# Turning rows by DMA instead of on TensorE in the block loop of a pre-norm state-space and mixture-of-experts kernel

## The reference

```python
# x: (2, 4096, 512)
def ssm(x):                                       # x is the layer-normalised input
    s = sigmoid(silu(x @ s_w1.T + s_b1) @ s_w2.T + s_b2)
    u = (x @ B_w.T + B_b) * s                     # 128 states
    h[t] = h[t-1] @ A.T + u[t]                    # scan over 4096 steps
    y = h @ C_w.T + C_b + x @ D_w.T + D_b
    return y * sigmoid(x @ g_w.T + g_b)

def moe(x):                                       # x is the layer-normalised x1
    chosen = argmax(x @ gate_w.T)                 # 8 experts
    return x + x @ expert_w[chosen].T

x1 = x + ssm(layernorm(x))
out = x1 + moe(layernorm(x1))
```

## Time and profile before

| | us |
|---|---|
| median of 3 runs | 1006.66 (1006.65 to 1008.63) |
| the profiled execution | 1007.09 |
| its span in the profile | 1005.3 |
| PE busy | 966.4 (96%) |
| DVE, ACT, POOL busy | 674.9, 408.1, 402.1 |

### The profile page before, as it was taken

The page is one execution under the profiler, slowest core; times in us unless marked ns, Lnnn a source line. Parts: engine busy times, 40 slices in busy tenths (PEclk is TensorE's granted clock), DMA queues, the critical chain, the costliest instruction groups (busy, mean ns, idle before and its releaser), DMA issues. The chain is left out here.

```text
span 1005.3 us, 16387 instructions
## 1 busy us (share of the span) xinstructions
PE 966.4 (96%) x5009; PEld 792.6 (79%) x5010; DVE 674.9 (67%) x1655; ACT 408.1 (41%) x704; POOL 402.1 (40%) x522
## 2 busy tenths in 40 slices
PE   7999999999999999999999999999857999999995
PEld 6788888888888888888888888888646888888884
DVE  6677777777777777777777687776985444444442
ACT  5333333333333333333333332332546666666662
POOL 1041616345261634626163362615273333333332
PEclk9999999999999999999999999999979999999998
DMA  9051022121302212130221203112265555555441
GB/s 322 12 178 43 22 105 79 48 86 42 126 32 95 83 44 88 40 126 33 95 84 43 97 31 126 41 44 85 84 220 178 159 160 166 168 159 161 138 149 55
DMA packets 47324, 101.70 MB, mean 101 GB/s; under 512 B 5781, under 2 KB 6549, under 8 KB 47264
## 3 DMA queue, kind: packets, MB, share of 16 engines
q1 hardware_dynamic: 33680, 61.93, 19.1%
q0 software_dynamic: 10800, 33.70, 8.7%
q10 hardware_dynamic: 2784, 5.31, 1.6%
HBM read 64.85 MB, written 37.90 MB: 102 GB/s over the span
## 5 line engine op out<-in xcount | busy, mean ns | idle before, releaser
L412 POOL TENSOR_TENSOR y_biased<-y_biased,gate 128x512 f32<-128x512 f32 x60 | 91.3, 1521 | 144.4 <-DVE y_biased L764 144.4
L481 POOL DMA_INDIRECT out<-gate,ids x71 | 69.9, 984 | 153.9 <-DVE gate L1029 115.2
L1355 PE MATMUL y<-expert_hi,x1T_hi 128*128 x284 | 119.3, 420 | 3.9 <-DVE x1T_lo L1023 3.9
L1029 DVE TENSOR_TENSOR gate<-y,x_rows 128x512 f32<-128x512 f32 x71 | 49.1, 691 | 108.2 <-PE y L1355 108.2
L1355 PE MATMUL y<-expert_hi,x1T_lo 128*128 x284 | 112.7, 397 | 0.0
L1355 PE MATMUL y<-expert_lo,x1T_hi 128*128 x284 | 112.3, 395 | 0.0
L1065 PE MATMUL gates<-GwT_hi,xT_hi 128*128 128x512 f32 x256 | 104.8, 409 | 0.0
L1065 PE MATMUL y<-DwT_hi,xT_hi 128*128 128x512 f32 x256 | 101.9, 398 | 0.5 <-DVE gateT L696 0.5
L1066 PE MATMUL gates<-GwT_lo,xT_hi 128*128 128x512 f32 x256 | 100.8, 394 | 0.0
L1067 PE MATMUL gates<-GwT_hi,xT_lo 128*128 128x512 f32 x256 | 100.3, 392 | 0.0
L1067 PE MATMUL y<-DwT_hi,xT_lo 128*128 128x512 f32 x256 | 100.3, 392 | 0.0
(11 more groups left out here) (246 smaller groups left out, 2372.8 us busy)
## 6 DMA issues: line engine op xcount, KB each, us to landing
x_rows<-routed_rows SPq DMA_DIRECT2D x71, 258.0 KB, 2.6
x_in<-L_attn_x SPq DMA_DIRECT2D x32, 512.0 KB, 4.4
x_rows<-L_attn_x SPq DMA_DIRECT2D x32, 512.0 KB, 4.4
raw_weights<-L_ffn_expert_w ACTq DMA_DIRECT2D x5, 1024.0 KB, 7.3
raw_weights<-L_ffn_expert_w SPq DMA_DIRECT2D x3, 1024.0 KB, 8.9
routed_rows<-padrow SPq DMA_DIRECT2D x9, 258.0 KB
out<-gate,ids POOLq DMA_INDIRECT x71, 2.8
raw_weights<-L_attn_D_w SPq DMA_DIRECT2D x1, 1024.0 KB, 8.1
```

The costliest lines, as they stand in the source:

```text
L412: nc.gpsimd.tensor_tensor(yb[:, i, :], yb[:, i, :], gate[:, i, :], ALU.mult).then_inc(S_["gated"], 1)
L481: nc.gpsimd.indirect_dma_start(out=out_rows, out_offset=bass.IndirectOffsetOnAxis(ap=ids[m][:, 0:1], axis=0), in_=res[m], in_offset=None, ...
L1029: nc.vector.tensor_tensor(res[m], Y[m % 2][:], rows[m][:, 0:D], ALU.add).then_inc(S_["slot_result"], 1)
L1355: ins = nc.tensor.matmul(Y[m % 2][:], x2T[a][:, k, m % 2 * P:(m % 2 + 1) * P], flat[w][:, bass.ds(first + k * D, D)], start=(k == 0 and a ...
```

## The change

In the block loop, from block 1 on, neither x_norm nor x1 is turned on TensorE. Instead each tile of 128x512 fp32 values is split into two planes of 16-bit halves (`halves`, 128x1024, two buffers), an SP DMA transposes it (`flipped`, two buffers), ACT joins the planes again to fp32 (`joined`, two buffers), and the high part is taken from that on ACT, the low part on POOL. The split is on ACT for x and on DVE for x1. The x_norm buffer goes: the normalised rows are written over x_in. One sequence number runs through all transposes: in block b the four tiles of x1 of block b-1, then the four of x of block b+1. So the tiles 0 to 2 of xT are written in the block before, each as soon as the gates products have read it; tile 3 follows at the next block's start, its low part on DVE. Block 0's own rows and the x1 of block 15 are turned on TensorE as before. The state products now open a block.

```diff
             xin, xn = sb("x_in", [P, NT, D]), sb("x_norm", [P, NT, D])   # before
+            xin = sb("x_in", [P, NT, D])
+            halves = [sb(f"halves{q}", [P, 2 * D], u16) for q in range(2)]
+            flipped = [sb(f"flipped{q}", [P, 2 * KD, P], u16) for q in range(2)]
+            joined = [sb(f"joined{q}", [P, KD, P]) for q in range(2)]
+        def planes(tile):
+            return tile.bitcast(u16).rearrange("p (d h) -> p h d", h=2)
+        def turn_x1(b, i):
+            return 2 * NT * b + NT + i
+        def turn_x(b, i):
+            return 2 * NT * (b - 1) + i
# SP
+            def load_x(b, n):
+                if b == 1:
+                    sp.wait_ge(S_["xT_psum"], NT)
+                elif b > 1:
+                    sp.wait_ge(S_["x_halves"], NT * (b - 2) + 2 * (n + 1))
+                sp.dma_start(xin[:, 2 * n:2 * n + 2, :], x_t[n][b]).then_inc(S_["xin_loaded"], 16)
+            def flip(n, made, count):
+                sp.wait_ge(made, count)
+                wait(sp, S_["joined"], n - 1)
+                sp.dma_start_transpose(flipped[n % 2][:], halves[n % 2][:]).then_inc(turned[n % 2], 16)
-            for b in range(3, NBLK):
-                load_x(b)
-                load_residual(b - 1, (b - 1) % 2, (b - 1) // 2)
-            load_residual(LASTB, 1, LASTB // 2)
+            for b in range(NBLK):
+                if b > 0:
+                    for i in range(NT):
+                        flip_x1(b - 1, i)
+                for n in range(NB):
+                    if b < LASTB:
+                        flip_x(b + 1, 2 * n)
+                        flip_x(b + 1, 2 * n + 1)
+                    if b + 2 < NBLK:
+                        load_x(b + 2, n)
+                    if n == 0 and b > 1:
+                        load_residual(b, b % 2, b // 2)
# POOL
+            def low_x1(b, i):
+                pool.wait_ge(S_["x2T_hi"], NT * b + i + 1)
+                hi, lo = [h[:, :, i % 2 * P:(i % 2 + 1) * P] for h in turned_rows(b, i)]
+                nc.gpsimd.tensor_tensor(lo, joined[turn_x1(b, i) % 2][:], hi.bitcast(f32), ALU.subtract
+                                        ).then_inc(S_["x2T_lo_pool"], 1)
+            # low_x(b, i): the same for xT
                 if b < LASTB:
                     rstd1(b + 1)
+                if b > 0:
+                    low_x1(b - 1, 0)
+                    low_x1(b - 1, 1)
+                    low_x1(b - 1, 2)
                 if b >= 2:
                     scatter(b - 2, q)
+                if b > 0:
+                    low_x1(b - 1, 3)
+                if b < LASTB:
+                    low_x(b + 1, 0)
                 if b > 0:
                     rstd2(b - 1, 1 - q)
+                if b < LASTB:
+                    low_x(b + 1, 1)
+                    low_x(b + 1, 2)
# ACT
+            def halve_x(b, i):
+                n = turn_x(b, i)
+                act.wait_ge(S_["xn_ready"], NT * b + i + 1)
+                wait(act, turned[n % 2], 16 * (n // 2))
+                nc.scalar.activation(halves[n % 2][:].rearrange("p (h d) -> p h d", h=2), planes(xin[:, i, :]), ACT.Copy
+                                     ).then_inc(S_["x_halves"], 1)
+            def join(n, freed, count):
+                act.wait_ge(turned[n % 2], 16 * (n // 2 + 1))
+                wait(act, freed, count)
+                nc.scalar.activation(planes(joined[n % 2][:].rearrange("p k t -> p (k t)")),
+                                     flipped[n % 2][:].rearrange("p (h k) t -> p h (k t)", h=2), ACT.Copy
+                                     ).then_inc(S_["joined"], 1)
+            # join_x1, join_x: join once the low part made of the buffer's last content is done
+            # high_x1, high_x: Copy of joined to x1T_hi, xT_hi (high_x waits for g_psum of its tile)
# ACT, a block's order after the change (t: tail of b-1; a: block b+1)
+                high_x(b, 3); gates(b - 1, 3)
+                # for m in 0, 1: sigmoid, siluT_hi
+                join_x1(b - 1, 0); high_x1(b - 1, 0); join_x1(b - 1, 1)
+                # select
+                high_x1(b - 1, 1); join_x1(b - 1, 2); high_x1(b - 1, 2)
+                normalise1(b + 1, 0); halve_x(b + 1, 0)
+                join_x1(b - 1, 3); high_x1(b - 1, 3)
+                normalise1(b + 1, 1); halve_x(b + 1, 1)
+                gates(b, 0); scoresT(b - 1, 0); join_x(b + 1, 0); high_x(b + 1, 0)
+                normalise1(b + 1, 2); halve_x(b + 1, 2); join_x(b + 1, 1)
+                normalise1(b + 1, 3); halve_x(b + 1, 3)
+                gates(b, 1); high_x(b + 1, 1); scoresT(b - 1, 1); join_x(b + 1, 2)
+                # h_last
+                gates(b, 2); high_x(b + 1, 2)
+                # h_hi
+                join_x(b + 1, 3)
# DVE
+            def halve_x1(b, q, i):
+                n = turn_x1(b, i)
+                dve.wait_ge(S_["x1_ready"], NT * b + i + 1)
+                wait(dve, turned[n % 2], 16 * (n // 2))
+                nc.vector.tensor_copy(halves[n % 2][:].rearrange("p (h d) -> p h d", h=2), planes(xrow[q][:, i, 0:D])
+                                      ).then_inc(S_["x1_halves"], 1)
                 for m in range(KH):
+                    if tail:
+                        halve_x1(old, oldq, m)
                     silu_product(b, m)
+                if tail:                       # behind ln1_mv
+                    halve_x1(old, oldq, 2)
+                    ln2_stats(old, oldq, 2)
                 u_in_pairs(b)
                 if tail:
-                    tail_lo(old, 0)
-                    tail_lo(old, 1)
+                    halve_x1(old, oldq, 3)
# TensorE
-                for i in range(NT):            # the turns of x_norm, now in block 0 alone
-                    ...
                 if tail:
                     y_state(b - 1)
                 for m in range(KH):
+                    if m == 0:
+                        wait(pe, S_["silu_ready"], KH * b)
+                    else:
+                        wait(pe, S_["g_sum"], NT * b)
                     pe.wait_ge(S_["xT_hi"], NT * (b + 1))
-                    pe.wait_ge(S_["xT_lo"], NT * (b + 1))
+                    pe.wait_ge(S_["xT_lo"], NT + b)
+                    wait(pe, S_["xT_lo_pool"], (NT - 1) * b)
-                    tail_turn(b - 1, 1 - q, 0)  # and 1, 2, 3 further on
```

More of the change, by code:

```diff
@@ L294, in _, with flip_x1, flip_x @@
         def _(sp):
-            def load_x(b):
-                wait(sp, S_["xn_ready"], NT * b)
-                for n in range(NB):
-                    sp.dma_start(xin[:, 2 * n:2 * n + 2, :], x_t[n][b]).then_inc(S_["xin_loaded"], 16)
+            def load_x(b, n):
[8 more added lines that the diff above has]
+                sp.dma_start_transpose(flipped[n % 2][:], halves[n % 2][:]).then_inc(turned[n % 2], 16)
+            def flip_x1(b, i):
+                flip(turn_x1(b, i), S_["x1_halves"], NT * b + i + 1)
+            def flip_x(b, i):
+                flip(turn_x(b, i), S_["x_halves"], NT * (b - 1) + i + 1)
             def load_residual(b, q, turn):
@@ new lines, in join, with join_x1 @@
+            def join(n, freed, count):
[4 more added lines that the diff above has]
+                                     ).then_inc(S_["joined"], 1)
+            def join_x1(b, i):
+                if i > 1:
+                    join(turn_x1(b, i), S_["x2T_lo_pool"], NT * b + i - 1)
+                elif i == 1:
+                    join(turn_x1(b, 1), S_["xT_lo"], NT + b + 1)
+                else:
+                    join(turn_x1(b, 0), S_["xT_lo_pool"], (NT - 1) * (b + 1))
@@ new lines, in join_x, with high_x1 @@
+            def join_x(b, i):
+                if i > 1:
+                    join(turn_x(b, i), S_["xT_lo_pool"], (NT - 1) * (b - 1) + i - 1)
+                else:
+                    join(turn_x(b, i), S_["x2T_lo_pool"], NT * (b - 2) + i + NT - 1)
+            def high_x1(b, i):
+                act.wait_ge(S_["joined"], turn_x1(b, i) + 1)
+                wait(act, S_["scoresT_psum"], 2 * (b - 1) + i // 2 + 1)
+                nc.scalar.activation(turned_rows(b, i)[0][:, :, i % 2 * P:(i % 2 + 1) * P], joined[turn_x1(b, i) % 2][:],
+                                     ACT.Copy).then_inc(S_["x2T_hi"], 1)
@@ L555, in body @@
                 ahead = b < LASTB
[L556 to L561 removed]
+                if tail:
+                    high_x(b, NT - 1)
+                    gates(b - 1, NT - 1)
+                else:
+                    for i in range(NT):
+                        act.wait_ge(S_["xT_psum"], i + 1)
+                        nc.scalar.activation(xT[0][:, :, i * P:(i + 1) * P], by_block(XT_BANKS[i]), ACT.Copy
+                                             ).then_inc(S_["xT_hi"], 1)
                     prep(1)
@@ L571, in body @@
                     nc.scalar.activation(sT[0][:, m, :], silu[:, m, :], ACT.Copy).then_inc(S_["silu_hi"], 1)
-                if not tail:
+                if tail:
+                    join_x1(b - 1, 0)
+                    high_x1(b - 1, 0)
```

(10 more changed lines are left out.)

178 lines of the change are left out of this document (100 added, 78 removed).

## The result

| | us |
|---|---|
| before, 4 runs beside it | 1007.19 (1006.65 to 1008.63) |
| after, 4 runs | 1054.15 (1049.48 to 1062.67) |
| ratio | 1.047 [1.041, 1.054] |
| profiled execution after, its span | 1053.97, 1052.2 |

The change costs 47 us. The forecast was 972 with a range of 950 to 1045: wrong in sign, and outside the range.

What follows compares the result with a forecast made beforehand. TensorE's own work was taken to bound the loop: 43.85 - 3.73 + 1.1 + 0.3 = 41.52 us a block, 35 us less over 15 blocks, so 972 us; 8-in-10 range 950 to 1045, forecast's own 963 to 985.

Steps and rivals of the forecast that it cites:

- What is removed, 3.73 us a block: TensorE's turns of x_norm and x1 and the gaps behind them in blocks 1 to 15, leaving 40.12 us without stalls.
- L = 3.6: Time in us from the end of a split on DVE to the start of its join on ACT.
- the second chain: Select, queued on ACT behind joins of x1, comes late before the scan: a stall of 0.3 us a block.
- The second and third rival: ACT's chain too late, 1019 to 1064 us, chance 0.27; DMA transposes the bound, above 44 us a block, chance 0.08.
- First chain, 1.1 us: Two x1 splits ahead of the silu products on DVE delay siluT_lo and s2: 1.1 us stall a block.
- h: Time of one x1 plane split on DVE, taken as 1.0 us, with 0.7 and 1.2 kept as ends.
- The rest of the block without a stall: Beyond both chains, joins, scoresT, low parts and state products were laid out as ready in time, adding no stall.
- the stall-free count: Rival with no stalls: 15 blocks of 40.12 us give back 56 us, 951 us in all, chance 0.10.

Runs made afterwards that it cites:

- e9: Changed kernel with low parts on DVE, splits of x1 tiles 0 and 1 on ACT, select behind one join, scoresT(1) before the last normalise: 967.0 us.
- e10: Changed kernel with splits of x1 tiles 0 and 1 on ACT, select behind one join, POOL's low parts cut to 2 columns of each 128: 964.7 us.
- e1: Changed kernel without the transposing DMAs, ACT's join reading the split halves directly: 1058.3 us.
- e2: Changed kernel with POOL's low parts cut to 2 columns of each 128, instructions, waits and order kept: 1009.9 us.
- e5: Kernel before the change with seven 128x512 subtractions a block added on POOL, on a buffer nobody else uses: 1041.5 us.

## Why the prediction was wrong, point by point

**What is removed, 3.73 us a block: right.** Blocks of e9 take 41.0 us on the mean, the shortest of e9 40.3 and of e10 40.2, where the prediction had 40.12 with no stall.

**L = 3.6: right for x1, and without effect.** 3.61 us measured from a split's end to the join for x1's last tile (3.5 in the middle of 15 blocks), and 3.14 at the most for tile 1, which the second chain was worked out for (396.63 to 399.77, ACT came without a wait); for tile 2 of x it was 4.9 to 7.4 us where ACT waited, above what the forecast allowed, and cost TensorE nothing. e1, with no transposing DMA at all, is no faster. The second and third rival were not it (that 1054 lies between the 1019 and 1064 which the second gives for L = 5 and 6 is chance: TensorE waits 1.0 us in all for scoresT): ACT does wait for flips (50.9 us before its joins), but no wait of PE in after is put down to a join or to the high part behind it, and the transposes are far from the bound. The join was taken at 1.0 us and takes 1.36, the split on ACT 1.06; none of this set a wait of TensorE.

**First chain, 1.1 us: right in place, half in size.** In the block from 385.10 siluT_lo ends 11.77 us after s1 starts (399.68 less 387.91), where the sum had 10.62. By the starts of the instructions, the two splits add 2.77 us instead of 2.0; both siluT_lo are longer by 0.87 (1.60 and 1.69 for 1.31 and 1.11); and DVE gains 1.3 in front of them instead of 0.85. 2.0 + 0.77 + 0.87 - 1.3 = 2.3. The mis-sized term is h, with what it does to siluT_lo. The prediction saw POOL at work there and its 1.11 us against 0.68, and counted it as part of that instruction's own length. It is a wait for a running instruction, so another instruction of DVE in that stretch pays it too. The split by itself takes 0.65 us, by the 0.66 to 0.69 of those that meet no POOL, below the h = 0.7 that I kept as the lower end.

**Second chain, 0.3 us: wrong.** Select was on time. The 2.0 us at z_half_lo come from two low parts of x1 on POOL at 402.96, which hold the addition of two elements (1.18 for 0.16) and the cast (1.32 for 0.30). These two alone are 2.04 us.

**The rest of the block without a stall: wrong, and this is the step that failed.** The sum has no term for it, and it measured 30.0 + 12.1 us of waits of TensorE for z_half_lo and chunk_ends. "POOL: 7 x 1.3 = 9 us on 19 busy: fits" and "no engine becomes the bound by its total; the order does it" ask whether POOL has time and whether its results are in time. Both held: TensorE waited for no low part. What the count left out is that DVE's copies, casts and two-source work stand still while POOL's large instructions run. e2 and e5 give the price from both sides: seven subtractions made nearly empty give 44 us of after back, seven pure ones a block, 103 in all, added to before cost 34. Per instruction that is 34 / 103 = 0.3 us of TensorE's time for each 1.3 us instruction on 128x512 put on a POOL that has room, in this kernel and at these places.

**The clock: not in the sum at all.** The earlier trace rows had 1.00 throughout, so no stall was priced above its length. In after 8 of 15 stretches of 45 us show 0.96, at about 1.5 us for one fall, of which a shorter wait for z_half_lo behind it gave most back in four blocks. In e2, without that wait, 11 falls cost their full 1.4 to 1.5 us.

**The whole.** The waits view has 31.0 + 30.0 + 12.1 us in 60 waits, plus 0.16 each for the hop, 83 us, or 5.5 a block; 40.12 + 5.5 + 0.8 for the clock = 46.4 of 46.79. About 0.4 us a block I can't place; small waits for scoresT and hT_lo are in it.

The prediction said that it would be wrong if the longest wait of PE were for x1T_lo, the scoresT turns or hT. It was none of them: all the places that I watched were the new path's own consumers, and the damage was on old instructions which the diff doesn't name. Of what it said the profile would show, the block starts (46.8 for 41.5) and the 0.3 us wait before the scan were wrong, and the wait put down to siluT_lo, the missing turns and the transposes' 3.5 us were right.

With the splits and the low parts placed as in e9, turning by DMA is worth 40 us, against 56 for the stall-free count.

## What to carry to other kernels

Before work is moved to POOL, list what DVE does in the same stretch: every DVE instruction with two SBUF sources, and every SBUF to SBUF copy or cast, can wait for a large POOL instruction that runs (here 1.3 us on 128x512), whatever its own size. A group whose instruction and operands are the same in both kernels and whose mean has nearly quadrupled (300 to 1116 ns) points at this faster than any wait does. And where PE has no slack, a stall of 2 us is priced with a possible fall of the clock behind it: it came behind 11 of 15 such stalls in e2 and behind 5 of 15 in after.

## What the runs showed of the hardware

- A DVE addition of two elements took up to 1.20 us and a copy of 16 elements up to 1.25, with POOL instructions of 1.3 us on 128x512 beside them; 0.16 and 0.13 alone. An addition with one source in PSUM took 0.43 inside a POOL instruction. Beside POOL's power of four elements (1.05 us) and its scatter issues (0.96 us) casts and two-source subtractions took what they take alone.
- A transposing DMA of 128x1024 two-byte elements, SBUF to SBUF, took 3.6 us from the end of the split to the start of the join, and up to 7.4 for the tile behind the loads. With 120 of them the profile page's DMA packets rise from 47324 to 174046, 132501 of them under 512 B, and the DMA share of the loop from 0.20 to 0.43; the load x_in of 512 KB took 3.9 us, where it took 4.4. The Trainium skill, page VectorE: DVE Perf Modes, section The three transpose paths, gives 1309 ns for one 128x128 transpose by DMA; eight of these in one DMA took 3.6 us with all hops and not eight times that.
- ACT writes 1024 two-byte elements with a stride in 1.36 us (the join) and reads them so in 1.06 us (the split); DVE's split takes 0.65.
- After a wait of 2.18 us TensorE's granted clock was 0.50 for about 3.5 us of products (e2); after waits of 2.14 us it fell in some blocks and not in others.
